# Head-size-8 attention on one core: the gather of softmax sums moved between the two halves of the stack spreads

## The reference

```
h = layernorm(x)                           # g, b
q, k, v = h @ wq, c @ wk, c @ wv           # c = h (self) or the context (cross)
                                           # 20 heads of size 8
a = softmax(q k^T * 8**-0.5)
x = (a v) @ wo + bo + x
```

## Time and profile before

| what | value |
|---|---|
| median of 3 runs | 4166.11 us (4163.22 to 4181.46) |
| profiled execution | 4149.92 us |
| its span, first to last instruction | 4148.1 us |
| mean granted clock of TensorE | 0.883 |
| PE busy | 3903.9 us, 94% |
| DVE busy | 2324.7 us, 56% |
| ACT busy | 2173.5 us, 52% |
| POOL busy | 1215.8 us, 29% |

### The profile page before, as it was taken

The page is one execution under the profiler, slowest core; times in us unless marked ns, Lnnn a source line. Parts: engine busy times, 40 slices in busy tenths (PEclk is TensorE's granted clock), DMA queues, the critical chain, the costliest instruction groups (busy, mean ns, idle before and its releaser), DMA issues. The chain is left out here.

```text
span 4148.1 us, 103517 instructions
## 1 busy us (share of the span) xinstructions
PE 3903.9 (94%) x38592; PEld 3363.6 (81%) x38592; DVE 2324.7 (56%) x4208; ACT 2173.5 (52%) x5452; POOL 1215.8 (29%) x1313
## 2 busy tenths in 40 slices
PE   5989879999998988999999999969999999999899
PEld 3766657777777987898888888858888888888799
DVE  3666634444434555666666666645556565555554
ACT  3665635555543445555555555535555555555344
POOL 4112111111104433333333333322222222232443
PEclk7888955555558999999999999989999999999999
DMA  3322212122111000000000000000000000000000
GB/s 99 90 75 71 76 46 69 47 57 56 53 37 30 0 19 23 1 0 0 0 0 0 0 0 0 1 23 3 2 2 2 2 2 2 2 2 1 16 19 21
DMA packets 97848, 98.23 MB, mean 24 GB/s; under 512 B 27664, under 2 KB 73104, under 8 KB 97680
## 3 DMA queue, kind: packets, MB, share of 16 engines
q1 hardware_dynamic: 94480, 94.50, 8.4%
q10 hardware_dynamic: 3200, 1.31, 0.1%
HBM read 20.76 MB, written 5.24 MB: 6 GB/s over the span
## 5 line engine op out<-in xcount | busy, mean ns | idle before, releaser
L1075 POOL TENSOR_TENSOR a_probs<-a_probs,a_rsums 128x1024 f32<-128x1024 f32 x160 | 303.7, 1898 | 750.4 <-DVE a_rsums L1173 750.4
L1095 ACT ACTIVATE a_probs<-a_scores_banks,a_negmax 128x128 f32<-128x128 f32 x1280 | 367.3, 377 | 297.4 <-DVE a_negmax L1161 297.4
L1075 POOL TENSOR_TENSOR c_probs<-c_probs,c_rsums 128x616 f32<-128x616 f32 x160 | 201.5, 1259 | 768.6 <-DVE c_rsums L1173 768.5
L1095 ACT ACTIVATE c_probs<-c_scores_banks,c_negmax 128x77 f32<-128x77 f32 x1280 | 313.2, 335 | 204.5 <-DVE c_negmax L1161 204.5
L1154 DVE COPY c_outT<-c_out_bank 128x512 f32<-128x512 f32 x160 | 110.7, 692 | 369.6 <-PE c_out_bank L1315 309.2
L1438 ACT ACTIVATE f_gate<-f_up_bank,bias 128x256 f32<-128x256 f32 x320 | 151.2, 473 | 286.4 <-PE f_up_bank L323 286.4
L1462 DVE SCALAR_TENSOR_TENSOR f_hidden<-f_up_bank,bias,f_gate 128x256 f32<-128x256 f32 x320 | 149.6, 481 | 254.3 <-ACT f_gate L1438 136.2
L1154 DVE COPY a_outT<-a_out_bank 128x512 f32<-128x512 f32 x160 | 110.7, 692 | 298.6 <-PE a_out_bank L1315 246.6
L686 ACT ACTIVATE c_probs<-c_scoresT_banks 77x1024 f32<-77x1024 f32 x160 | 163.1, 1019 | 175.3 <-PE c_scoresT_banks L805 175.2
L1161 DVE TENSOR_REDUCE a_negmax<-a_scores_banks 128x4 f32<-128x512 f32 x320 | 206.2, 686 | 73.8 <-PE a_scores_banks L1216 73.8
L743 DVE TENSOR_REDUCE a_negmax<-a_scores_banks 128x8 f32<-128x1024 f32 x160 | 194.8, 1218 | 90.3 <-PE a_scores_banks L788 89.1
(11 more groups left out here) (340 smaller groups left out, 11912.9 us busy)
## 6 DMA issues: line engine op xcount, KB each, us to landing
a_q_stack<-a_q_compact SPq DMA_DIRECT2D x96, 160.0 KB
a_k_stack<-a_k_compact SPq DMA_DIRECT2D x96, 160.0 KB
c_q_stack<-c_q_compact SPq DMA_DIRECT2D x96, 160.0 KB, 3.1
c_k_stack<-c_k_compact SPq DMA_DIRECT2D x96, 96.2 KB, 2.8
x_tokens<-in_x SPq DMA_DIRECT2D x16, 320.0 KB, 5.3
a_out<-a_heads SPq DMA_DIRECT2D x64, 80.0 KB, 2.6
c_out<-c_heads SPq DMA_DIRECT2D x64, 80.0 KB, 2.0
out_x<-x_tokens SPq DMA_DIRECT2D x32, 160.0 KB, 1.9
```

Source lines behind the costliest of these rows:

```text
L1075: nc.gpsimd.tensor_tensor(probs[i][:], probs[i][:], rsums[(k - 1) % 2][:].unsqueeze(2).broadcast_to([P, UNIT, NK]), ALU.mult).then_inc(s_p ...
L1095: done = nc.scalar.activation(probs[i][:, h, :], scores[:, h // GROUP, h % GROUP * NK:(h % GROUP + 1) * NK], ACT.Exp, bias=negmax[k % 2][: ...
```

## The change

Two statements move; nothing is added or taken away. On SP the gather of sums, with its wait for the heads copies, now stands at the head of the branch for step 6, ahead of the six spreads of half 1 and behind the six of half 0. On VectorE the reciprocal, with its wait for the gather, goes from step 8 to step 9, where it stands behind the reduction of step 9. Both hold for a0 and c0. The wide stages are the same.

```diff
                         sp.wait_ge(s_ctxT, ahead)
                     sp.dma_start(ctx_in[0:NK, :, :], source).then_inc(s_ctx_in, 16)
+                if s == 6 and live(prev, QUADS):
+                    sp.wait_ge(s_heads, GROUPS * (prev + 1))
+                    sp.dma_start(sums[:], heads[(local - 1) % 2][1:P:32, :, :]).then_inc(s_sums_in, 16)
                 if s in (5, 6) and live(nxt, QUADS):
                     half, par = s - 5, (local + 1) % 2
...
                             sp.dma_start(stack[par][64 * half + c:64 * (half + 1):SPREAD, :, 0:source.shape[-1]].bitcast(F32), source)\
                                 .then_inc(s_stack[half], 16)
-                if s == 6 and live(prev, QUADS):
-                    sp.wait_ge(s_heads, GROUPS * (prev + 1))
-                    sp.dma_start(sums[:], heads[(local - 1) % 2][1:P:32, :, :]).then_inc(s_sums_in, 16)
                 if s == 8 and live(prev, QUADS):
...
-                if s == 8 and live(quad_of(q, k) - 1, QUADS):
+                if s == 9 and live(quad_of(q, k) - 1, QUADS):
                     dve.wait_ge(s_sums_in, 16 * quad_of(q, k))
                     nc.vector.reciprocal(sums[:], sums[:]).then_inc(s_rsums, 1)
```

## The result

| | kernel before | changed kernel |
|---|---|---|
| median | 4164.66 us (4159.23 to 4181.46, 4 runs) | 4100.86 us (4090.15 to 4103.47, 4 runs) |
| profiled execution | 4149.92 us | 4102.62 us |

The ratio is 0.983 (95% interval 0.9802 to 0.9858): 64 us faster by the medians, 47 us by the two profiled executions. The forecast was 4083 with a range of 4055 to 4135.

The account below looks back on a forecast made before the run. It took a0 to be bound by VectorE's wait for the gather of sums, idling TensorE and lowering its clock. 79.2 + 3.6 + 3.2 - 3 = 83 us off the median 4166.11 gave 4083 us, range 4055 to 4135.

Parts of the forecast that it names:

- The wait and its removal: In a0, VectorE's reciprocal waits 3.46 us a quad for the gather of sums; moving both statements removes this, side costs 0.
- Idle time is paid twice: In a0, TensorE's stop costs itself and then half clock behind it; 99 us of 412 ran at half clock.
- The clean quad of 25.6 us: An a0 quad at full clock without its own 1.76 us of idle time: 27.35 - 1.76 = 25.6 us.
- the first term of the sum: In a0, all 13 quads between first and fourteenth gather fall from 31.69 to 25.6 us: 79.2 us gained.
- the 3 us set against it for the first quad: Deduction because a0's clock was already at 0.50 before the first gather: 0 to 4.3 us, taken as 3.
- The quad that I took as the pattern: The a0 quad from 206.09 to 233.44, wholly at clock 1.00: 27.35 us for 400 matmuls.
- the time from 237 to 240 without any TensorE: Idle time in the a0 quad at 233, read as bringing the granted clock to 0.50 at 241 to 244.
- a clock that still falls: Rival: in a0 the waits go but the clock falls once a quad; only 33 us won, 4133; chance 0.15.
- the granted clock of the stretch: Sign of being right: clock of 0.97 or more over a0's 13 quads, with gathers about 25.6 us apart.
- quads of 28 us or more with the clock at 0.50: Sign of being wrong: a0 quads this long, with the clock at 0.50 after the projections.
- two or three quads that still fall to half clock: Allowance on the slow side of the range 4060 to 4110: 4.3 us each, and their idle time.
- The fourteenth stall and quad 15: End of a0: 3.6 us for the stall outside the 13 quads, 3.2 us for quad 15 regaining clock.

Follow-up runs that it names:

- e2: Changed kernel with only the gather of sums moved, the reciprocal back in step 8: 4104.85 us, ratio 0.9856 to the kernel before.
- e8: Changed kernel with both small attention loops written out, plus one VectorE fill of 3072 elements in each a0 quad: 4098.81 us.
- e7: Changed kernel with both small attention loops written out, plus one VectorE fill of 1024 elements in each a0 quad: 4065.89 us.
- e9: Kernel before with the loops of a0 and c0 written out, nothing moved: 4140.90 us, ratio 0.9956.
- e5: Changed kernel with the loops of a0 and c0 both written out: 4057.88 us, ratio 0.9768 to the kernel before.
- e4: Changed kernel with only the self-attention (a0) loop written out: 4084.10 us, ratio 0.9809 to the kernel before.
- e10: Changed kernel with the c0 loop written out and a0's in part, leaving two returns in a0: 4079.50 us, ratio 0.9800.
- e11: Changed kernel with only the c0 loop written out, leaving four returns in a0: 4101.55 us, ratio 0.9857.
- e1: The changed kernel once more, as measure for the other kernels of its chip: 4096.28 us, ratio 0.9846 to the kernel before.

## Why the prediction was right, and where it was off

**The wait and its removal: shown.** The gather was issued between the halves, its wait on heads held no spread up (0.95 us early in the quad shown), it landed in time and the reciprocal was hidden. All of this is as priced, at 0. When exactly it landed no row tells, since nothing waited for it; in e2 it was at most 4.9 us behind the issue. e2 shows more: the gather alone did as much, as far as the intervals can tell.

**Idle time is paid twice: shown.** e8 puts 14.3 us of idle time back by another cause and loses 40.6, while e7, with a fill that stays covered, loses nothing in the stretch. e9, the kernel before without a loop, has 395.22 - 367.13 = 28.1 us of idle time in the stretch, 25.4 more than e5, and is 64.4 us longer. The clean quad of 25.6 us was right: 25.8 in the changed kernel, 25.4 in e5.

**The step that failed is the first term of the sum,** "13 x (31.69 - 25.6) = 79.2 us". It let all thirteen quads become clean. Nine of them, those without a return, took 30.8 us before and take 25.9 now. The four with a return, the quads that hold the waits for "issue", took 33.7 us before and take 34.7 now: they gained nothing. The stretch fell by 39.6 us, where the term, with the 3 us set against it for the first quad, said 76. Part of the mean of 31.69 from which the term starts was the price of the returns, which the change does not touch: where nothing loops the stretch fell by 64.4 us (395.2 to 330.8), and only the change and the written out loops together give 81.2 (412.0 to 330.8). In the changed kernel the returns cost 372.4 - 330.8 = 41.6 us of the stretch.

The mistake was in the reading. The quad that I took as the pattern, 206 to 233, has no return in it. The next one has: the time from 237 to 240 without any TensorE, of which the prediction spoke, lies at a return. Two rows of the kernel before, in order of time, VectorE and TensorE at that place:

```profile
238.08 1.16 DVE L743 TENSOR_REDUCE a_negmax<-a_scores_banks 128x8 f32<-128x1024 f32 x1
```

```profile
240.25 0.33 PE L788 MATMUL a_scores_banks<-a_k_stack,a_q_stack 31*128 31x128 f32 x2 [3.63 <-DVE a_negmax L743]
```

The bracket puts all 3.63 us down to VectorE, but the reduction ended at 239.24 and the scores began 1.01 us later; in the quad of the earlier trace rows, without a return, it was 499.19 - 499.14 = 0.05 us. The wait for the sums lay over the larger part of the stop at the return. The wait that took the place of the removed one was thus none of the rivals, though it had the price of one of them, a clock that still falls, in four quads of thirteen. The quad taken as the pattern was rare in another way too: of the twelve stops of 1.3 us and more in the stretch before, its stop of 1.76 us is the only one behind which the clock stayed up. Two signs that the prediction had named told of it: the granted clock of the stretch is 0.92 where 0.97 or more was to be, and quads of 28 us or more with the clock at 0.50, its sign of being wrong, came four times.

**How the time still came near: in part luck.** The range allowed for two or three quads that still fall to half clock, at 4.3 us each and their idle time. That was meant for chance falls, and it covered part of a cause that had not been seen. The first quad and the small terms came out better than priced, by which executions were profiled or by chance.

**What stops TensorE at a return.** That it is the return is shown by e4, e5, e10 and e11. That it is the fetch of instructions fits the rows: two packets on the instruction queue within 4 us at each of the four stops and nowhere else in the stretch (with the loop written out, e5, no window of 4 us holds two), and an unedited loop (c0 in e4) that gets four stops when the code ahead of it becomes longer. It was not measured by itself. The Trainium skill (Runtime: NRT & Kernel Launch, Instruction fetch mechanics) says that fetch ahead is sequential, in blocks, and that a taken branch to a block that is not held must be fetched by DMA first; it gives no time. Here the whole stop was 3.1 to 3.7 us and 1.1 to 2.0 us more some 3 us later, and in c0 it was there or not by the place of the loop.

**The small terms.** The fourteenth stall and quad 15 were priced at 3.6 + 3.2 = 6.8 us; from the fourteenth gather to c0's first load it is 69.8 us for 79.1, 9.3 less. The first quad, for which 3 us were set against the gain, took 34.6 us before and 24.8 in the changed kernel's profile, but 29.2 in e1's and 33.2 in e2's: it can be clean or wholly slow, and in the profile compared here it was clean. c0 was priced at 0 and is 673.9 us for 671.6; e1, the same kernel, has 671.6.

**The offset of the profile.** By profiles the forecast was 4067 and the measurement 4102.6, 36 us more; by medians 4083 and 4100.9, 18 more. The kernel before was profiled in an execution 15 us under its median and the changed one in an execution 2 us over; so about half of the 36 us does not show in the medians. That is owed to which executions were profiled, and not to the reasoning.

## What to carry to other kernels

When a wait is removed, look at what lies under it: an idle time that a profile gives to one releaser can cover a second one on the same engine, and the tell-tale was that the engine started 1.0 us after its releaser had ended. Compare repeats by their place in the loop before one of them is taken as the clean pattern, since a quad with the branch back and one without are not the same work. Where TensorE's clock falls behind a stop, as here behind six of twelve stops of 1.1 us (e8) and behind every one of 2 us and more in the self-attention, the stops cost two to three times their length (41.6 us for 19.4 us of idle time by the returns, 64.4 for 25.4 by the wait, 40.6 for 14.3 by the fill), and a loop of few iterations may be cheaper written out, but this moves the loops behind it, which must be measured too.

## What the runs showed of the hardware that was not expected

- A return of a loop cost 7 to 11 us in a0 and nothing or some 4 us in c0, with the same five iterations. c0 without a loop and wholly at half clock took 677.8 us (e10); with its loop it took 671.6 to 673.9 where one patch ran at full clock, and 687.4 and 694.8 in the two kernels in which only the code ahead of it had been written out.
- Two stops of TensorE of the same length, in the same place of the same loop-free code, are followed by 13 us at half clock or by none (e8).
- c0 stays at a granted clock of 0.50 although TensorE is busy all the time (250.00 of the 250 us from 750 to 1000 in the kernel before), with no stop ahead of it. In eleven of the thirteen profiled executions one patch there, in e8 two, ran above it for 10 to 25 us: some 450 us behind the stage's first load in five of them, elsewhere in the others. Most quads that such a patch fills took about 36 us for 39.4. Without stops at its returns c0 took 658.5 (e8) to 677.8 us (e10). How much of the scatter of single executions comes from this is not shown, since one execution of each kernel was profiled.
